# One solve in place of two in the delta-rule attention: one matmul of 64 columns gives what two of 32 columns gave

## What is computed

```python
v = v * beta[..., None]
kb = k * beta[..., None]            # k has unit length here
attn = -jnp.einsum('bhncd,bhned->bhnce', kbc, kc) * strict_lower
for i in range(1, chunk):
    upd = jnp.einsum('...j,...ji->...i', attn[..., i, :], attn[..., :, :i])
    attn = attn.at[..., i, :i].add(upd)
attn = attn + jnp.eye(chunk, dtype=q.dtype)
u = attn @ vc
w = attn @ kbc
# then, from chunk to chunk, with a state S:
ui = ui - wi @ S
oi = qi @ S + a_loc @ ui
S = S + jnp.einsum('bhcd,bhcv->bhdv', ki, ui)
```

## Time and profile before

| what | value |
|---|---|
| timed, median of 3 (range) | 974.75 us (974.1 to 976.68) |
| profiled execution, first to last instruction | 1008.6 us |
| mean granted TensorE clock of the profiled execution | 0.913 |
| PE busy | 878.8 us, 87%, 11,862 matmuls and as many weight loads |
| DVE busy | 553.4 us, 55% |
| ACT busy | 385.0 us, 38% |
| POOL busy | 482.9 us, 48% |
| attention, from its first matmul of line 1337 to the end of stage 3 | about 300 to 790 us of the span |

### The profile page before, as it was taken

One profiled execution on the slowest core, in us unless ns is written; L12 is line 12 of the kernel. 1 busy time (PEld: TensorE's weight loads), 2 busy tenths in 40 slices (PEclk: granted clock), 3 DMA queues, 4 the chain that ended last, 5 costly groups with the idle time before them and its releaser, 6 DMA issues. The chain is left out here.

```text
span 1008.6 us, 28139 instructions
## 1 busy us (share of the span) xinstructions
PE 878.8 (87%) x11862; PEld 766.9 (76%) x11862; DVE 553.4 (55%) x1680; ACT 385.0 (38%) x790; POOL 482.9 (48%) x589
## 2 busy tenths in 40 slices
PE   7466999999948878998899889997987789999996
PEld 6346999999936656786667666775676689999996
DVE  6554656555445844657285834474247256666662
ACT  5323444444215322365236523461145244444441
POOL 2568999355620012382118711783134343445667
PEclk8577999999977798999999999997687799999999
DMA  9823677443140110011001120011001544434644
GB/s 302 124 75 79 202 231 231 138 138 99 48 126 1 23 29 17 4 22 51 16 4 31 35 77 24 18 41 51 26 24 64 173 131 147 129 119 114 119 84 45
DMA packets 75466, 86.08 MB, mean 85 GB/s; under 512 B 9752, under 2 KB 62148, under 8 KB 74317
## 3 DMA queue, kind: packets, MB, share of 16 engines
q1 hardware_dynamic: 61132, 63.74, 21.5%
q0 software_dynamic: 14208, 20.55, 8.9%
HBM read 46.70 MB, written 34.01 MB: 80 GB/s over the span
## 5 line engine op out<-in xcount | busy, mean ns | idle before, releaser
L998 DVE TENSOR_TENSOR e_hid<-e_sg,e_pu 128x320 f32<-128x320 f32 x256 | 125.0, 488 | 173.3 <-ACT e_sg L939 130.0
L939 ACT ACTIVATE e_sg<-e_pg 128x320 f32<-128x320 f32 x256 | 112.0, 438 | 222.2 <-PE e_pg L896 189.4
L894 PE MATMUL e_pg<-e_xlo,e_whi 128*128 128x320 f32 x256 | 97.2, 380 | 12.4 <-DVE e_hid L998 6.5
L282 POOL DMA_INDIRECT queue<-wide_rows,slot x64 | 66.5, 1039 | 83.1 <-DVE slot L478 26.3
L882 PE MATMUL e_po<-e_expert,e_hid 128*128 128x128 f32 x640 | 84.0, 275 | 1.3 <-DVE e_hid L998 1.3
L882 PE MATMUL e_po<-expert,e_hid 128*128 128x128 f32 x640 | 84.4, 275 | 0.5 <-issue 0.5
L882 PEld LDWEIGHTS e_po<-e_expert,e_hid 128*128 128x128 f32 x640 | 79.9, 191 | 2.0 <-DVE e_hid L998 1.8
L882 PEld LDWEIGHTS e_po<-expert,e_hid 128*128 128x128 f32 x640 | 80.3, 191 | 0.8 <-issue 0.7
L895 PE MATMUL e_pg<-e_xhi,e_wlo 128*128 128x320 f32 x256 | 80.1, 313 | 0.0
L896 PE MATMUL e_pg<-e_xhi,e_whi 128*128 128x320 f32 x256 | 79.8, 312 | 0.0
L896 PE MATMUL e_pu<-e_xhi,e_whi 128*128 128x320 f32 x256 | 79.8, 312 | 0.0
(11 more groups left out here) (351 smaller groups left out, 2180.2 us busy)
## 6 DMA issues: line engine op xcount, KB each, us to landing
expert<-wexp_in SPq DMA_DIRECT2D x14, 512.0 KB
e_expert<-wexp_in SPq DMA_DIRECT2D x14, 512.0 KB
line<-blank SPq DMA_DIRECT2D x3, 1310.0 KB
e_xs<-queue SPq DMA_DIRECT2D x12, 327.5 KB, 5.8
e_xs<-line SPq DMA_DIRECT2D x6, 647.5 KB, 6.1
expert<-wexp_in SPq DMA_DIRECT2D x14, 256.0 KB
e_expert<-wexp_in SPq DMA_DIRECT2D x14, 256.0 KB
queue<-blank SPq DMA_DIRECT2D x2, 1310.0 KB, 10.0
```

The source lines that it names most:

```text
L282: pool.indirect_dma_start(io.queue, bass.IndirectOffsetOnAxis(ap=k.slot[:, j, 1:2], axis=0), k.xn[:, j, :], None, bounds_check=SLOTS - 1, ...
L894: pe.matmul(out, whi[par][:, i, fs], xlo[par][:, cols], start=True, stop=False)
L939: act.activation(sg[n % 2][:], pg[n % 2][:, 0:HALF], ACT.Silu).then_inc(silued, 1)
L998: dve.tensor_tensor(hid[q % 2][:, f, c * HALF:c * HALF + HALF], sg[n % 2][:], pu[n % 2][:, 0:HALF], ALU.mult).then_inc(hidden, 1)
```

## The change

The inverse no longer begins with ones on its diagonal but with beta / |k|^2. Every step of `substitute` is linear in the columns, so that what comes out is the inverse with its columns scaled. The values are scaled by |k| in place of beta / |k|. Then the same 32x32 matrix gives u and w, and one matmul takes keys and values as one moving operand of 2 x 32 columns: `kn` and `vh` become parts of one tile `kv` in the order keys of even groups, values, keys of odd groups. `prepare_keys` goes, and with it `solve_w`, `weighted` and the wait of `betas`. The product for w now comes out untransposed, so that `keep_w` transposes while it copies. A half of a solve fills two banks (two chunks each), and both `keep_u` and `keep_w` become two instructions; VectorE reads the banks only behind ScalarE.

```diff
-        kn = [sb(f"kn{i}", [P, NCH, SEQS, DH]) for i in range(2)]
-        vh = sb("vh", [P, NCH, SEQS, DH])
+        kv = sb("kv", [P, 3, NCH, SEQS, DH])
+        kn, vh = [kv[:, 0], kv[:, 2]], kv[:, 1]
...
+        U_AT = lambda g: 1 - g % 2
+        halves_of = lambda g, t: [bank.rearrange("p (m t c) -> p m t c", t=2, c=CHUNK)[:, :, t, :]
+                                  for bank in (pp[:, 2, :], po[:, 1, :])]
...
                 steps.done(pool.memset(inv[:], 0.0))
-                steps.done(pool.memset(inv[:].rearrange("p a b -> p (a b)")[:, 0:CHUNK * CHUNK:CHUNK + 1], 1.0))
...
                 if j == 0:
                     pe.wait_ge(silued, UNITS * a + 4)
                     behind(pe, ukept, 2 * a)
+                    behind(pe, wkept, 2 * a)
...
-            def solve_values(g, half):
+            def solve(g, half):
                 if half:
                     pe.wait_ge(ukept, 2 * g + 1)
+                    pe.wait_ge(wkept, 2 * g + 1)
                 else:
                     pe.wait_ge(prepared, g + 1)
                     pe.wait_ge(vready, g + 1)
                     pe.wait_ge(masked, QUARTERS * g + QUARTERS)
                     behind(pe, oscaled, 2 * g)
...
-            def solve_keys(g, half):
...
                     behind(pe, crossed, 2 * g)
                 for i in range(HCH):
                     n = half * HCH + i
+                    bank = po[:, 1, :] if i >= HCH // 2 else pp[:, 2, :]
                     for s in range(SEQS):
-                        at = (i * SEQS + s) * CHUNK
+                        at = (i % (HCH // 2) * SEQS + s) * 2 * DH
                         for h in range(H):
-                            mm = pe.matmul(po[strip(h), 1, at:at + CHUNK], kn[g % 2][strip(h), n, s, :],
-                                           solve_w[strip(h), n * SEQS + s, :], start=True, stop=True)
-                mm.then_inc(wsolved, 1)
+                            mm = pe.matmul(bank[strip(h), at:at + 2 * DH].rearrange("p (t c) -> p t c", t=2),
+                                           solve_by[strip(h), n * SEQS + s, :],
+                                           kv[strip(h), g % 2:g % 2 + 2, n, s, :], start=True, stop=True)
+                mm.then_inc(solved, 1)
...
             def factors(a):
+                dve.wait_ge(subchain, blanks(a))
+                dve.transpose(both(inv[:])[:, 0:CHUNK * CHUNK:CHUNK + 1], bvk[:, 1, :])
                 dve.wait_ge(masked, QUARTERS * a + QUARTERS)
                 dve.transpose(both(nmat[:]), both(low[:])).then_inc(factored, 1)
...
-            def prepare_keys(a):
-                dve.wait_ge(prepared, a + 1)
-                dve.tensor_tensor(solve_w[:], solve_u, bc(bvk[:, 1, :].unsqueeze(2), [P, NH, CHUNK]),
-                                  ALU.mult).then_inc(weighted, 1)
...
             def keep_w(g, half):
-                dve.wait_ge(wsolved, 2 * g + half + 1)
-                dve.tensor_copy(flat(wT[:, half * HCH:half * HCH + HCH, :, :]), po[:, 1, :]).then_inc(wkept, 1)
+                dve.wait_ge(ukept, 2 * g + half + 1)
+                for i, part in enumerate(halves_of(g, 1 - U_AT(g))):
+                    n = half * HCH + i * (HCH // 2)
+                    last = dve.transpose(flat(wT[:, n:n + HCH // 2, :, :]), part)
+                last.then_inc(wkept, 1)
...
             def keep_u(g, half):
-                act.wait_ge(usolved, 2 * g + half + 1)
-                act.activation(u[:, half * HCH:half * HCH + HCH, :, :].rearrange("p n s d -> p (n s d)"), pp[:, 2, :],
-                               ACT.Copy).then_inc(ukept, 1)
+                act.wait_ge(solved, 2 * g + half + 1)
+                for i, part in enumerate(halves_of(g, U_AT(g))):
+                    n = half * HCH + i * (HCH // 2)
+                    last = act.activation(u[:, n:n + HCH // 2, :, :].rearrange("p n s d -> p (n s) d"), part, ACT.Copy)
+                last.then_inc(ukept, 1)
```

More of the change, by code:

```diff
@@ L1197, in attention, with blanks @@
         block = ctx.enter_context(nc.Block(no_gpsimd_drain=True))
+        INVERT_STEPS = 1 + 2 * (CHUNK - 1)
+        U_AT = lambda g: 1 - g % 2
+        halves_of = lambda g, t: [bank.rearrange("p (m t c) -> p m t c", t=2, c=CHUNK)[:, :, t, :]
+                                  for bank in (pp[:, 2, :], po[:, 1, :])]
+        def blanks(a):
+            return 2 + (a - 1) * INVERT_STEPS if a else 1
         @block.sync
@@ L1261, in invert @@
             def invert(a):
-                steps = Steps(pool, subchain, 2 + (a - 1) * 64 if a else 0)
+                steps = Steps(pool, subchain, blanks(a) - 1)
                 pool.wait_ge(ksummed, a + 1)
                 steps.done(pool.memset(inv[:], 0.0))
-                steps.done(pool.memset(inv[:].rearrange("p a b -> p (a b)")[:, 0:CHUNK * CHUNK:CHUNK + 1], 1.0))
                 if not a:
@@ L1272, in invert @@
                         put(a - 2, PUT_AT.index(j), PUT_AT.index(j) + 1)
-                assert steps.n == 64
+                assert steps.n == INVERT_STEPS
                 pool.sem_inc(inverted, 1)
@@ L1491, in read @@
                     pe.wait_ge(wkept, 2 * g + 2)
+                    pe.wait_ge(ukept, 2 * g + 2)
                 for s in range(SEQS):
@@ L1667, in slot @@
                             at["keys"] = keys(a, 0, KEYS_BEFORE)
-                        solve_values(g, 0)
+                        solve(g, 0)
                     large(f, 0)
-                    if here and not f:
-                        solve_keys(g, 0)
                     if behind_it and f in (1, 2):
@@ L1674, in slot @@
                     if here and f == 1:
-                        solve_values(g, 1)
-                    if here and f == 3:
-                        solve_keys(g, 1)
+                        solve(g, 1)
                     if behind_it and f == 4:
@@ L1841, in betas @@
                 dve.wait_ge(tanhed, 2 * a + 2)
-                behind(dve, wsolved, 2 * a)
                 link(dve.transpose(both(nmat[:]), both(low[:])))
@@ L1862, in invert_first @@
             def invert_first(first, last):
-                dve.wait_ge(subchain, 2)
                 dve.wait_ge(factored, 1)
@@ L2145, in stage @@
                     low_rows(g + 2, 0)
-                if ahead:
-                    prepare_keys(a)
                 if later:
```

19 lines of the change are left out of this document (9 added, 10 removed).

## The result

The changed kernel takes 952.37 us (median of 4 runs, 950.6 to 955.39), the kernel before, run beside it, 975.71 us (4 runs, 974.1 to 978.06). The ratio is 0.9757 [0.9722, 0.9793]: 23.3 us shorter, where 9.2 had been forecast. In this profiled execution the span is 953.5 us and the execution's own time 955.39 us, that is 2 us above its span. That is the first thing to see: an execution's span is no longer than its time, so recording is no explanation of the 33.9 us. Which chip this result comes from is not on record.

What follows compares the result with a forecast made beforehand. PE was taken to bound the attention stages, stalled for instructions around the solves. 1.3 us of streaming plus 9.2 of stalls less 1.6 added gave 8.9 us: 974.75 to 965.8, say 965.5; range 947 to 976 us.

Steps and rivals of the forecast that it cites:

- the 33.9 us: Gap by which the timed median lay below the profiled span of 1008.6 us, taken as time absent from timed runs.
- The third: Solves and updates: a third of 27.6 us of instruction stalls counted for timed runs, 9.2 us, bounds 0 and 23.6.
- The clock, left out: PE's clock dropping behind stalls of instruction supply costs extra time; left out of the sum, no size given.
- the first rival: Timed runs lose as much to instruction supply in the solves as the profiled one: 951 us, down to 945; chance 0.24.
- The trickle and the long stalls: PE's old solves: few matmuls between 0.47 us idles, suspected profiler-only; single idles of 1.15 us, expected in timed runs too.
- Streaming: PE's solves without stalls, eight halves of 64 columns instead of sixteen old ones: 1.3 us won.
- Slower, by the clock: Merged halves at 1.2 GHz lose 0.42 us each; all eight there give 979.8 us; chance 0.09 including a new wait.
- Stalls that stay: Instruction waits left in the merged solves and updates of the profiled execution: about 4 us, bounds none and 8.
- Added: Split copies of u and w and the diagonal's transpose, on PE's way: 1.6 us lost, at most 4.
- Removed at no gain, new waits not met: `prepare_keys`, 4 x 1209 ns of VectorE, never delayed PE; second solve and first gram won't wait for copies.
- Passed on: GpSimd's 51.8 us inverse chain is no floor under the stage; it starts earlier by what the solves save.
- Nothing to win: Supply keeps up in timed runs, so 1.3 - 1.6 leaves +0.3: 975 us, within 972 to 977; chance 0.19.

Runs made afterwards that it cites:

- the recorded kernel before: The kernel before, unedited, profiled once more: 972.72 us, with a span of 970.4 us.
- the doubled product: The kernel before with the multiplication by the weights in `prepare_keys` done twice in each group: 976.19 us, ratio 1.0009 to the kernel before.
- the split: The changed kernel with every 64-column matmul of the merged solve issued as two of 32 columns: 982.65 us, ratio 1.0096 to the kernel before.
- the early matmuls: The changed kernel with a single-column matmul before each merged-solve matmul: 985.15 us, ratio 1.009 to the kernel before (third chip); 1029.29 us on the second.
- late: The changed kernel with as many single-column matmuls at the stage ends: 960.0 us, ratio 0.9861 to the kernel before (third chip); 1001.66 us on the second.

## Why the prediction was wrong

**The third.** The mechanism and the sign were right; the step that failed is "I count a third of the 27.6 us for the timed runs, 9.2 us". It rested on "the profiled execution holds time that the timed ones don't". Every execution whose own time is on record has a span 2 to 3 us under it, and the recorded kernel before, 972.72 us, has 15.7 us of waits for instructions. Of these the change removes 14.4 us, where 9.2 were counted. The 33.9 us were most likely one chip against another, times of one beside a span of the other.

**The clock, left out.** The second step that failed is "(A stall also costs clock behind it; I leave that out.)". The 14.4 us of waits, the 2.6 us of streaming below and nothing else would be 17.0 us; 23.3 were measured. Where the other 6 us come from is shown only in part: at the start of stage 0 the granted clock rises from 0.79 to 1.00.

**The near hit of the first rival.** "All stalls are real" said 951 us, and 952.37 was measured. That is in good part luck. It took 23.6 us of stalls off, from the 27.6 of an execution of 1008.6 us; in the recorded kernel before the old halves hold 30.9 us, not 45.8, and 14.4 us of waits went. What filled the gap is streaming, twice the 1.3 us counted, and the time that it did not count, the clock among it. The table that goes with a profile needs the same execution's own time; where that is missing, a gap to the median is an unknown, and not an argument for taking two thirds off the largest term.

**The trickle and the long stalls.** The prediction had said that the long stalls "should be there in both, and without a trickle they grow". They do: on the faster chip 15.7 us in 18 waits and no trickle, the longest single one in front of the solves 1.6 us against 1.1. It named this and then gave it no number.

**Streaming.** 1.3 us won was forecast. With 1.94 us and 3.58 us a half it is 12 x 1.21 + 4 x 1.71 - 6 x 1.94 - 2 x 3.58 = 2.6 us. One reading under it was wrong: of the twelve halves counted at 2.4 GHz one, at 376.8 us, has a granted clock of 0.50. The gram's form was a good stand-in, 6 to 7% dear. Two of eight halves ran at 1.2 GHz, so the rival "Slower, by the clock" stayed far from its five.

**Stalls that stay.** About 4 us, at most 8, were forecast for the profiled execution. On the fast chips 1.3 and 2.5 us were found. But the forecast was made for an execution with the trickle, and there it failed: with the merge the halves still take 34.2 us, where six at 1.94 and two at 3.58 would be 18.8. The trickle is not a matter of the count alone.

**Added.** u, w and the diagonal came at 772, 851 and 219 ns against 754, 850 and 193. The timed cost on the path, 1.6 us forecast, can't be told apart. Splitting the matmuls again with all of these edits kept loses 8.6 us against before, but that holds the denser placing of the solves as well.

**Removed at no gain, new waits not met.** Both held: no trace of the kernel before has a wait of PE for the weights' product, no wait of PE for a copy of u or w stands before a solve or a gram in the trace of the changed kernel, and the second solve began in stage 1 behind a big matmul with no wait in front of it.

**Passed on.** The gain came through the inverse in stages 0 and 1 (6.6 and 6.5 us) but less in stages 2 and 3 (3.3 and 4.5). The statement that the chain "is no floor" was right for what begins it and overlooked what is in it: with six `put`s in it the inverse was already late, so it could hold part of the gain back. In stage 2 VectorE waits 3.8 us instead of 2.3, and PE at its longest 3.2 instead of 1.7; that the merge did this is not shown, since the doubled product has the same wait. Stages 2 and 3 also begin with a merged half at 1.2 GHz of 3.58 us. Two old ones were counted at 3.42; in stage 2 of the recorded kernel before they took 1.93 and 1.22, the second at full clock. Taking the `put`s out gave 8.8 us more.

**"Nothing to win", and the skill.** The Trainium skill, in "Runtime: NRT & Kernel Launch", section "Instruction fetch mechanics", has the refill mostly hidden. On the third chip the same eight packets cost 7.7 us among big matmuls and 32.9 among small ones. So the trace agrees with that sentence among big matmuls, where 0.5 us of waits are left, and not among small ones. What decides is the count of instructions in a stretch against one packet in 3.3 to 4.0 us. With 23.3 us for the change, 30 for the split, 32.9 for the early matmuls and each stall ending behind a packet, the cause is shown from both sides for the fast chips.

**What stays open.** Why one chip has waits of 0.45 us between every few matmuls, why it is 4% slower, and what the change alone gives there. What sets the interval of 3.8 us is not shown either, but the trace of the recorded kernel before has a hint. Its first stall in stage 0, of 1.13 us, stands behind the first packet in 24 us, so no rate was exhausted there. And in 13 of the 18 waits 3.3 to 4.0 us pass from the start of the 128th matmul before it to the one that waited, while the packet starts 0.8 to 1.8 us after the former. So it looks as if a packet were asked for only when PE enters the one before it, and were then 3.3 to 4.0 us away; no run tested this. And the 6 of the 23.3 us that are neither waits nor streaming.

## What to carry to other kernels

Small matmuls are paid by the instruction, not by the column, wherever a stretch of a list asks for more than one packet of 256 instructions (loads counted) in some 3.8 us: count them per stretch, and make fewer and wider ones. Moving the halves by a slot within the stretch gave nothing back here. Compare a span with the own time of the same execution before crediting a difference to the profiler. When a stage gets shorter, look at what it waits for at its end: here a serial chain on GpSimd held DMAs, and issuing them elsewhere gave 8.8 us.

## What the runs showed of the hardware

- The same program takes 974 and 975 us on two chips and 1016 on a third. On the slow one waits for instructions of 0.3 to 0.5 us stand after every few matmuls in part of the solves; on the others no such series stands. Where the single-column matmuls stand counts on both kinds: early against late differs by 27.6 us on the slow chip and by 25.2 on the fast.
- Where PE waited for instructions, one packet of 256 took 3.3 to 4.0 us from its first to the next one's first instruction in 13 of 18 waits of the recorded kernel before, and up to 5.7 in the others. A half of the old solve uses one up in 1.2 us. PE went on 1.2 to 1.5 us after the end of a packet.
- A stall can cost twice: in the first 16 us of the solves of stage 0, behind stalls of 1.13 and 1.46 us, the granted clock was 0.79, and 1.00 in the changed kernel. In stage 1 the clock stayed at 1.00 through stalls of 1.15, 0.88 and 1.23 us.
